# Two layers' modulation on one core: the first layer's rows stored and read back ahead of later weights, the second layer's steps placed further down

## What is computed

```python
mod = (silu(c) @ wmod).reshape(8, 6, 1, 256)        # c: 8 x 256, wmod: 256 x 1536; one pair per layer
sa, ca, ga, sb, cb, gb = mod[:, 0], ..., mod[:, 5]
ga = (2 * (ga >= 0) - 1) * maximum(abs(ga), 0.25)   # gb likewise
h = layernorm(x) * (1 + ca) + sa
x = x + ga * attention(h)      # layer 0: norm, q/k/v/gate products, softmax; layer 1: a state-space block
h = layernorm(x) * (1 + cb) + sb
x = x + gb * ffn(h)            # layer 0: shared and routed experts; layer 1: ternary MLP
```

## Time and profile before

| | |
|---|---|
| runs, us | 2625.68 (median), 2636.82, 2623.66 |
| the profiled execution, us | 2636.68 |
| its span, us | 2634.9 |
| busy share: TensorE, VectorE, ScalarE, GpSimd | 87%, 66%, 51%, 50% |
| mean granted TensorE clock | 0.935 of full speed |

### The profile page before, as it was taken

The page is one execution under the profiler, slowest core; times in us unless marked ns, Lnnn a source line. Parts: engine busy times, 40 slices in busy tenths (PEclk is TensorE's granted clock), DMA queues, the critical chain, the costliest instruction groups (busy, mean ns, idle before and its releaser), DMA issues.

```text
span 2634.9 us, 26906 instructions
## 1 busy us (share of the span) xinstructions
PE 2303.8 (87%) x8452; PEld 1462.8 (56%) x8452; DVE 1735.8 (66%) x2782; ACT 1353.0 (51%) x1793; POOL 1316.8 (50%) x1135
## 2 busy tenths in 40 slices
PE   2799989999898986678998998998998988998978
PEld 1456657566575652235665555555555555565666
DVE  3445454554545449899689689689689689688730
ACT  0233425334253354546766766766766765766622
POOL 1232332522324215556667666666666666667833
PEclk6899999999999997888999998998999998999989
DMA  8034564455444464444555544655554644546622
GB/s 267 0 109 151 162 194 156 141 161 159 155 137 137 126 219 118 129 127 132 171 141 134 172 144 132 170 142 133 170 142 136 174 139 126 170 136 172 192 72 91
DMA packets 253773, 384.77 MB, mean 146 GB/s; under 512 B 19168, under 2 KB 159984, under 8 KB 253632
## 3 DMA queue, kind: packets, MB, share of 16 engines
q1 hardware_dynamic: 223408, 281.33, 36.9%
q0 software_dynamic: 30224, 101.73, 12.5%
HBM read 345.93 MB, written 47.55 MB: 149 GB/s over the span
## 4 chain that ended last, share of the span: by engine, by line
PE 51%; DVE 17%; issue 11%; ACT 10%; POOL 4%; DMA 2%; DVEq 0%; another core or an unknown queue 0%; POOLq 0%; SPq 0%; ACTq 0%
PE bank L235 27%; PE bank L241 7%; PE bank L1494 7%; PE bank L242 7%; DVE bank L1416 4%; DVE w_st L1424 4%; POOL d_in L1406 2%; DVE cv L1236 2%; ACT bank L1472 1%; DMA bc<-bc_rows 1%; ACT L1472 1%; DVE mid L1596 1%; PE bank L1052 1%; POOL f1L L1572 1%; ACT L1645 1%
## 5 line engine op out<-in xcount | busy, mean ns | idle before, releaser
L1406 POOL TENSOR_TENSOR d_in<-u,bc 128x512 f32<-128x512 f32 x512 | 661.8, 1303 | 386.6 <-DMA bc<-bc_rows 300.6
L1416 DVE TENSOR_TENSOR_SCAN bank<-bank,d_in 128x512 f32<-128x512 f32 x512 | 624.9, 1222 | 98.7 <-ACT bank L1472 71.3
L1494 PE MATMUL bank<-w_st,ident 128*128 128x512 f32 x1024 | 540.4, 642 | 93.2 <-DVE w_st L1424 92.9
L1472 ACT ACTIVATE bank<-dt,a_neg 128x512 f32<-128x512 f32 x512 | 348.0, 690 | 463.4 <-DVE w_st L1424 461.6
L1424 DVE TENSOR_TENSOR w_st<-bank,bc 128x512 f32<-128x512 f32 x512 | 345.2, 674 | 120.7 <-PE bank L1494 120.4
L241 PE MATMUL bank<-f1H,w_ring 128*128 128x512 f32 x768 | 361.6, 471 | 60.9 <-ACT raw L1305 22.4
L1494 PEld LDWEIGHTS bank<-w_st,ident 128*128 128x128 f32 x1024 | 197.8, 202 | 310.2 <-DVE w_st L1424 177.2
L242 PE MATMUL bank<-f1L,w_ring 128*128 128x512 f32 x768 | 312.0, 406 | 0.0
L205 POOL TENSOR_TENSOR norm_rstd<-norm_veps,minus_half 128x4 f32<-128x4 f32 x24 | 25.7, 1072 | 423.2 <-DVE norm_veps L201 423.0
L241 PE MATMUL bank<-f0H,w_ring 128*128 128x512 f32 x512 | 228.4, 446 | 3.6 <-POOL f0L L1572 3.6
L1572 POOL TENSOR_TENSOR f0L<-mid,f0H 128x512 fp32r<-128x512 f32 x128 | 170.0, 1329 | 122.7 <-DVE f0H L1600 86.6
(11 more groups left out here) (202 smaller groups left out, 3846.5 us busy)
## 6 DMA issues: line engine op xcount, KB each, us to landing
bc<-bc_rows SPq DMA_DIRECT2D x256, 512.0 KB, 5.0
w_ring<-w_units POOLq DMA_DIRECT2D x160, 512.0 KB, 4.2
w_exp<-L_ffn_ew SPq DMA_DIRECT2D x240, 256.0 KB, 4.6
eo_rows<-eo SPq DMA_DIRECT2D x56, 256.0 KB, 4.5
xs<-xs_rows SPq DMA_DIRECT2D x24, 512.0 KB, 4.0
w_units<-h_T SPq DMA_DIRECT2D x16, 512.0 KB
xA<-L_attn_x SPq DMA_DIRECT2D x8, 512.0 KB, 6.1
x_mid<-xA SPq DMA_DIRECT2D x8, 512.0 KB
```

The source lines that it names most:

```text
L1406: pool.tensor_tensor(d_in[:, nth(b, s) % IN, :], u[:, c, :], rows_tile(b, use)[:, 0, :], ALU.mult).then_inc(in_made.sem, 1)
L1416: dve.tensor_tensor_scan(bank[:, :], bank[:, :], d_in[:, nth(b, s) % IN, :], 0.0, ALU.mult, ALU.add).then_inc(scanned.sem, 1)
L1472: act.activation(state_bank(b, s)[:, :], dt[:, c, :], ACT.Exp, scale=a_neg[:, c, n:n + 1]).then_inc(dA_made.sem, 1)
L1494: pe.matmul(y_bank(c)[:, :], ident[:, :], w_st[:, nth(b, s) % WG, :], start=False, stop=(n == NST - 1)).then_inc(summed.sem, 1)
```

## The change

SP stores layer 0's rows (`store_rows(0)`) right behind the q/k weights, waits for that store, loads rowsA[0] and gate_rows[0], and only then issues w_hid and everything after it. Layer 1's rows are stored at the end of SP's setup (`store_rows(1)`), followed by a wait for both stores. VectorE's setup does only layer 0's steps (`modulation_vector(0)`, 17 instructions: three copies, two additions, and for each gate the same six steps as before, on 8 x 256). Layer 1's 17 instructions stand at place 40.5, behind block 0's second norm and ahead of the q/k biases. The 24 transposes stand on TensorE at place 62, behind the last q-k product and ahead of the output product; the two copies stand on VectorE at place 63, ahead of the reciprocal, whose place is the same. ScalarE's first feed-forward activation now also waits for both stores, since its output lies over `rows`.

```diff
 PLAN_A = dict(
+    rows_l1=0.5, rows_turn=22,
@@ setup_sync
+            MOD_STEPS = 3 + 2 + 2 * 6
+                def store_rows(l):
+                    sp.wait_ge(mod_step.sem, MOD_STEPS * (l + 1))
+                    sp.dma_start(mod_rows[l].rearrange("b j d -> b (j d)"), rows[:, l, :]).then_inc(mod_stored.sem, 16)
...
+                store_rows(0)
+
+                sp.wait_ge(mod_stored.sem, 16)
+                sp.dma_start(rowsA[0][:, :, :], mod_rows[0, 0, 0:3].partition_broadcast(P)).then_inc(rowsA_in.sem(0), 16)
+                sp.dma_start(gate_rows[0][:, :, :], mod_rows[0, 0, GB:GB + 1].partition_broadcast(P)).then_inc(rowsA_in.sem(0), 16)
                 sp.dma_start(w_hid[:, :, :], k_tiles(ins["L0_attn_W_hidden"])).then_inc(hid_weights_in.sem, 16)
...
-                sp.wait_ge(mod_step.sem, MOD_STEPS)
-                for l in range(2):
-                    sp.dma_start(mod_rows[l].rearrange("b j d -> b (j d)"), rows[:, l, :]).then_inc(mod_stored.sem, 16)
...
+                store_rows(1)
+                sp.wait_ge(*mod_stored.all(0))
-            MOD_STEPS = 6 + 4 + 2 * 6
@@ setup_tensor
-                pe.wait_ge(mod_step.sem, MOD_STEPS)
+            def rows_tensor():
+                yield x1_at(0) + PLAN_A["rows_turn"]
                 for l in range(2):
+                    pe.wait_ge(mod_step.sem, MOD_STEPS * (l + 1))
                     bank = banks[6 + l]
                     for j in range(NMOD * KD):
                         i = pe.transpose(bank[:, j * B:(j + 1) * B], rows[:, l, j * P:(j + 1) * P], ident[0:B, 0:B])
@@ setup_vector
+                modulation_vector(0)
+            def modulation_vector(l):
+                first = MOD_STEPS * l
+                for c in range(3):
+                    dve.wait_ge(mod_made.sem, 3 * l + c + 1)
+                    dve.tensor_copy(rows[:, l, c * 512:(c + 1) * 512], banks[1 + 3 * l + c][0:B, :]).then_inc(mod_step.sem, 1)
+                dve.wait_ge(mod_step.sem, first + 3)
+                for which in (CA, CB):
+                    r = rows[:, l, which * D:(which + 1) * D]
+                    dve.tensor_scalar(r, r, 1.0, None, ALU.add).then_inc(mod_step.sem, 1)
+                done = first + 5
                 for which in (GA, GB):
-                    r = rows[:, :, which * D:(which + 1) * D]
+                    r, s, m = rows[:, l, which * D:(which + 1) * D], sgn[:, l, :], mag[:, l, :]
...
+            def rows_vector():
+                yield x1_at(0) + PLAN_A["rows_l1"]
+                modulation_vector(1)
+                yield x1_at(0) + PLAN_A["rows_turn"] + 1
                 for l in range(2):
                     dve.wait_ge(modT_turned.sem, l + 2)
                     dve.tensor_copy(mod_T[:, l, :, :].rearrange("p b j -> p j b"),
@@ att_sync(b)
                 if b:
                     sp.dma_start(xA[b % 3][:, :, :], x_in_v[b]).then_inc(x_in.sem(b), 16)
                 else:
-                    sp.wait_ge(*mod_stored.all(0))
+                    return
@@ ffn_scalar(b), b == 0 and k == 0
                         act.wait_ge(modT_made.sem, 2)
+                        act.wait_ge(*mod_stored.all(0))
@@ the merged programs
-            in_order(*first_layer(att_tensor, ffn_tensor, experts_tensor), hastened(front_tensor(0)), ...
+            in_order(stretched(rows_tensor()), *first_layer(att_tensor, ffn_tensor, experts_tensor), hastened(front_tensor(0)), ...
-            in_order(*first_layer(att_vector, ffn_vector, experts_vector), stretched(decay_rates_vector()), ...
+            in_order(stretched(rows_vector()), *first_layer(att_vector, ffn_vector, experts_vector), stretched(decay_rates_vector()), ...
```

More of the change, by code:

```diff
@@ L480, in setup_vector @@
                                 ).then_inc(cT_made.sem, 1)
[L481 to L489, removed]
@@ L490, in setup_vector @@
-                done = 10
+                modulation_vector(0)
[9 more added lines that the diff above has]
+                done = first + 5
@@ L491, in setup_vector @@
                 for which in (GA, GB):
-                    r = rows[:, :, which * D:(which + 1) * D]
+                    r, s, m = rows[:, l, which * D:(which + 1) * D], sgn[:, l, :], mag[:, l, :]
                     dve.wait_ge(mod_step.sem, done)
-                    dve.tensor_scalar(sgn[:, :, :], r, 0.0, 2.0, ALU.is_ge, ALU.mult).then_inc(mod_step.sem, 1)
-                    dve.tensor_scalar(mag[:, :, :], r, -1.0, None, ALU.mult).then_inc(mod_step.sem, 1)
+                    dve.tensor_scalar(s, r, 0.0, 2.0, ALU.is_ge, ALU.mult).then_inc(mod_step.sem, 1)
@@ L497, in setup_vector @@
+                    dve.tensor_scalar(m, r, -1.0, None, ALU.mult).then_inc(mod_step.sem, 1)
                     dve.wait_ge(mod_step.sem, done + 2)
-                    dve.tensor_tensor(mag[:, :, :], mag[:, :, :], r, ALU.max).then_inc(mod_step.sem, 1)
+                    dve.tensor_tensor(m, m, r, ALU.max).then_inc(mod_step.sem, 1)
                     dve.wait_ge(mod_step.sem, done + 3)
-                    dve.tensor_scalar(mag[:, :, :], mag[:, :, :], 0.25, None, ALU.max).then_inc(mod_step.sem, 1)
@@ L501, in setup_vector @@
-                    dve.tensor_scalar(sgn[:, :, :], sgn[:, :, :], -1.0, None, ALU.add).then_inc(mod_step.sem, 1)
+                    dve.tensor_scalar(m, m, 0.25, None, ALU.max).then_inc(mod_step.sem, 1)
+                    dve.tensor_scalar(s, s, -1.0, None, ALU.add).then_inc(mod_step.sem, 1)
                     dve.wait_ge(mod_step.sem, done + 5)
-                    dve.tensor_tensor(r, sgn[:, :, :], mag[:, :, :], ALU.mult).then_inc(mod_step.sem, 1)
+                    dve.tensor_tensor(r, s, m, ALU.mult).then_inc(mod_step.sem, 1)
@@ L539, in att_sync @@
                 sp.dma_start(rowsA[b % 2][:, :, :], mod_rows[0, b, 0:3].partition_broadcast(P)).then_inc(rowsA_in.sem(b), 16)
-                if b == 0 or b == B - 1:
+                if b == B - 1:
                     return
@@ L1702, in adaln_kernel @@
             setup_tensor()
-            in_order(*first_layer(att_tensor, ffn_tensor, experts_tensor), hastened(front_tensor(0)), *(front_tensor(b) for b in every[1:]),
+            in_order(stretched(rows_tensor()), *first_layer(att_tensor, ffn_tensor, experts_tensor), hastened(front_tensor(0)), *(front_tensor(b) for b in every[1:]),
                      *(core_tensor(b) for b in every), *(mlp_tensor(b) for b in every))
@@ L1716, in adaln_kernel @@
             setup_vector()
-            in_order(*first_layer(att_vector, ffn_vector, experts_vector), stretched(decay_rates_vector()),
+            in_order(stretched(rows_vector()), *first_layer(att_vector, ffn_vector, experts_vector), stretched(decay_rates_vector()),
                      hastened(front_vector(0)), *(front_vector(b) for b in every[1:]), *(core_vector(b) for b in every), *(mlp_vector(b) for b in every))
```

## The result

The changed kernel takes 2599.82 us (median of four runs, 2598.94 to 2602.11), the kernel before beside it 2626.17 (2623.66 to 2636.82): ratio 0.9888, 95% interval 0.9867 to 0.9909. It is faster by 26.4 us; 27.9 were forecast for the median.

The account below looks back on a forecast made before the run. TensorE's chain bounds the whole run, but early on everything waits for rowsA's landing; 28.6 us earlier less 0.7 lost gives 27.9, so 2625.7 - 27.9 = 2597.8 us, range 2590 to 2612.

Parts of the forecast that it names:

- The bound: Start of block 0: everything behind the first product with a row, at 55.81 us, waits for rowsA; 28.6 us earlier.
- Layer 0's rows ready at 19.7: VectorE's setup: two additions done at 15.9 us, two gates 3.8 more, so ready at 19.7 against 27.4.
- Store and load: SyncE's setup: store lands in 2.0 us, rowsA and gate_rows in 5.4, landed at 27.2 instead of 55.8.
- SyncE's queue: Transfers behind the pair: w_hid to bout_row at most 6.9 us, SP free at about 55, 4 later; cost nil.
- Layer 1's steps: VectorE between second norm and first q/k bias: 6.4 us fill the 6.37 us hole; cost nil, at most 6.4.
- The copies: VectorE ahead of the reciprocal, behind the moved transposes: the copies end late, 0.7 us lost.
- The clock: TensorE ahead of the output product: half clock may stay up, 3.1 us more; left at nil in the sum.
- The rival with the clock up: Output product: transposes in the idle time keep full clock, gain 31.0 us, 2594.7 us; chance 13%.
- The sum: Whole kernel: 28.6 - 0.7 = 27.9 us gained, 2597.8 us from the median.
- A slow store and load: SyncE's setup: store landing 5.4 us, broadcast read 8.1, gain only 21.8, 2603.9 us; chance 12%.
- SyncE's new wait: End of SP's setup: waiting for layer 1's rows holds up xA[1] past 117 us; at 128, 2636.9 us; chance 3%.
- The base: Whole kernel: gain applied to the three runs' median, 2625.7 us, not the profiled 2636.7, which would give 2608.8.

Follow-up runs that it names:

- the second profile of before: The unchanged kernel before, profiled once more with no edit: 2628.69 us, span 2627.0, one run.

## Why the prediction was right, point by point

*The bound.* That everything hung on the first use of the rows was right: VectorE's later instructions, the end of block 0, and against the second profile of before the end of the span, moved by 27 to 30 us.

*Layer 0's rows ready at 19.7.* They are ready at 20.08; the third copy started 0.34 late. From its end to the last step there are 4.38 us (15.70 to 20.08); 4.34 were reckoned (15.36 to 19.7).

*Store and load.* 2.0 us were taken for the store's landing, 2.11 measured. 5.4 for the pair, 5.26 measured. First use at 27.48, predicted 27.2; 28.3 us earlier, predicted 28.6.

*SyncE's queue.* Predicted free at about 55, and xA[1] issued near 54: 53.56. No weight became a releaser. The remark that w_hid to bout_row would take up to 6.9 us was too careful: 2.2 (23.06 to 25.22). The likely reason is the quieter queue: the DMA engines' busy share was 0.19 from 20.1 to 22.2 us, and at full (1.05 by the profile) while w_hid was issued before (6.4 to 9.2). Most of that was used up further down, where the four zero fills took 12.19 us to issue instead of 8.97.

*Layer 1's steps.* 6.4 us predicted, 6.71 measured (34.52 to 41.23); the two additions took 0.96 us, where layer 0's took 0.48. GpSimd was at work on h_tok until 37.03 beside them, but that this slowed them was not tested. The first bias starts at 41.31 against 40.7 reckoned. It cost nothing, as said: the kernel with layer 1's steps in front of the first norm has the same distance from the first use to the last bias (31.00 to 50.55 is 19.55; here 19.46).

*The copies.* Predicted 0.7 lost; next to nothing, 0.03, measured: ScalarE ends the last exponential at 77.04 and the reciprocal starts at 77.10; before it was 0.03 behind (104.56, 104.59). The 24 transposes take 1.65 us at full clock, 0.6 of the time at half, and end early enough. This term was mis-sized: no row stood behind "the least I would take is 0.5", and by half of the 2.72 us in the earlier trace rows the copies would have ended at about 104.6, when the reciprocal started anyway.

*The clock.* Not in the sum. Against the first profile of before, the q/k products took 9.41 us instead of 8.59 and the first half of the output product 6.9 instead of 6.5, both because the clock came back later, and so 28.3 us at the first use became 27.1 at L636 (114.26 to 87.16). This is not a cost of the change: in the second profile of before the q/k products took 9.36 us, and from the reciprocal to L616 there are 10.06 us there as here. The rival with the clock up did not come true, and its price of 3.1 was right (3.0 measured with products in the gap).

*The sum, and luck.* Against the second profile the gain is 29.4 us up to the end of block 0, about 1 of which is the later clock of that execution's first products. So the forecast of 27.9 was a little low for what the change does, by the 0.7 us for the copies. That the measured medians differ by 26.4 us, only 1.5 from the forecast, is in part luck: on another chip it was 27.8, and the total moves by several us between executions of one kernel.

*The other rivals.* A slow store and load would have needed 5.4 and 8.1 us; they took 2.11 and 5.26. SyncE's new wait held nobody: xA[1] went out at 53.56, far ahead of 117.

*The base.* To apply the gain to the median and not to the one profiled execution was right. The spans of the two first profiles differ by 36.1 us; 9 of that lie behind the end of block 0's attention, where both kernels have the same work.

## What to carry to other kernels

When the whole kernel hangs on one small value made at its start, follow that value through every queue it passes: here the rows were stored at 27.45 us and read back only at 50.85, behind transfers of which the first to be needed, w_router, is read at 127.45 us. Splitting shared work so that the urgent half goes first paid in full here, because the other half fitted an idle stretch of its engine; put in front instead it cost 3.5 us. The idle time of that stretch in the trace (6.37 us) said beforehand that it would about fit. Below some 5 us, judge by the trace at a fixed instruction soon behind the edit and not by the total, which here moves by as much from one execution to the next.

## What the runs showed that was not expected

TensorE's transposes of 128 x 128 held the full clock as well as products did. The length of a first-layer block, 106.9 to 111.4 us, changes between executions and between neighbouring blocks with nothing changed in the code, in part with the time at half clock. Already the twelve first product records took 6.68 to 8.20 us in different executions, which moves everything behind them. Splitting the broadcast load brought the first 256 KB in 3.1 us instead of 5.26 for the whole pair of loads (512 KB).
